# Three of four chunks of the experts' second layer by parts, one high part cast on GpSimd, and a tail that runs one unit later

## What is computed

```python
x = x + attention(layernorm(x))          # 16 heads, weights (eps + |q - k|)^-2, gated
x = x + experts(layernorm(x))            # 8 experts, top 2, 128 -> 512 -> 128, relu
x = x + linear_attention(layernorm(x))   # 16 heads of 8, relu(q), relu(k) with decay
x = x + f(layernorm(x))                  # 384 of 512 tokens: gelu(x @ w_block); the others: x itself
```

## Time and profile before

| | |
|---|---|
| median of 3 runs | 1418.41 us (1417.85 to 1419.69) |
| profiled execution | 1417.84 us, its span 1416.1 us |
| mean TensorE clock granted | 0.997 of full |
| busy: TensorE, VectorE, ScalarE, GpSimd | 1385.1, 1091.4, 1099.4, 840.5 us |

### The profile page before, as it was taken

How to read it: one execution, slowest core, us unless ns; L and a number is a source line. 1 busy time by engine, 2 the same in 40 slices (tenths; PEclk the granted TensorE clock), 3 DMA queues, 4 the chain that set the end, 5 groups by cost and what they waited for, 6 DMA issues and landing times.

```text
span 1416.1 us, 18228 instructions
## 1 busy us (share of the span) xinstructions
PE 1385.1 (98%) x6488; PEld 742.1 (52%) x6488; DVE 1091.4 (77%) x2045; ACT 1099.4 (78%) x947; POOL 840.5 (59%) x657
## 2 busy tenths in 40 slices
PE   8999999999999999999999999899999999999996
PEld 4444444444444444444444444445777777777775
DVE  7887897788888887887888778635687686776857
ACT  2799789979978979979979979944676676766761
POOL 4568777777778778868877877411333333434330
PEclk9999999999999999999999999999999999999999
DMA  3000110111101101101101012443011010110100
GB/s 114 1 17 16 31 39 17 23 31 32 25 16 46 24 17 36 34 17 31 39 16 32 16 25 58 124 143 107 1 68 56 12 68 1 68 61 8 68 1 16
DMA packets 45705, 54.99 MB, mean 39 GB/s; under 512 B 13808, under 2 KB 32368, under 8 KB 44464
## 3 DMA queue, kind: packets, MB, share of 16 engines
q1 hardware_dynamic: 45616, 53.84, 13.0%
HBM read 48.97 MB, written 4.85 MB: 38 GB/s over the span
## 4 chain that ended last, share of the span: by engine, by line
PE 86%; DVE 8%; ACT 5%; issue 1%; DMA 0%; POOL 0%; SPq 0%; DVEq 0%; POOLq 0%
PE sc L406 14%; PE av L419 13%; PE z L74 12%; PE pj L74 12%; PE y L1214 8%; PE sc L401 6%; PE y L74 5%; PE pj L383 4%; PE pj L451 4%; DVE w L597 3%; PE pj L429 2%; ACT w L684 1%; ACT w L688 1%; ACT w L680 1%; DVE high L565 1%
## 5 line engine op out<-in xcount | busy, mean ns | idle before, releaser
L597 DVE TENSOR_SCALAR w<-sc 128x1024 f32<-128x1024 f32 x256 | 301.3, 1218 | 67.7 <-PE sc L406 66.4
L680 ACT ACTIVATE w<-w 128x2048 f32<-128x2048 f32 x128 | 237.6, 1904 | 121.5 <-DVE w L597 121.2
L320 POOL TENSOR_TENSOR wsum<-wsum,w 128x512 f32<-128x512 f32 x248 | 318.0, 1282 | 19.4
L969 POOL TENSOR_TENSOR hr_l<-hr,hr_h 128x512 fp32r<-128x512 f32 x112 | 151.9, 1357 | 261.6 <-ACT hr L1025 261.6
L406 PE MATMUL sc<-query,key 64*128 64x512 f32 x1024 | 241.7, 591 | 0.0
L684 ACT ACTIVATE w<-w 128x2048 f32<-128x2048 f32 x128 | 240.1, 1899 | 0.4
L688 ACT ACTIVATE w<-w 128x2048 f32<-128x2048 f32 x128 | 239.8, 1897 | 0.0
L419 PE MATMUL av<-w,vt 128*64 128x512 f32 x1024 | 233.8, 598 | 2.5 <-ACT w L688 2.4
L1025 ACT ACTIVATE hr<-z,b 128x512 f32<-128x512 f32 x256 | 173.4, 684 | 67.7 <-PE z L74 67.7
L306 POOL TENSOR_TENSOR sqq<-query 128x512 f32<-128x512 f32 x63 | 65.6, 1042 | 182.8 <-DVE query L537 137.1
L317 POOL TENSOR_TENSOR wsum<-w 128x512 f32<-128x512 f32 x124 | 159.3, 1285 | 5.2 <-ACT w L688 5.2
(11 more groups left out here) (214 smaller groups left out, 2360.7 us busy)
## 6 DMA issues: line engine op xcount, KB each, us to landing
hT<-head_recips SPq DMA_DIRECT2D x64, 256.0 KB, 4.0
rb<-routing SPq DMA_DIRECT2D x8, 2048.0 KB, 7.1
w<-in_W SPq DMA_DIRECT2D x16, 256.0 KB, 5.4
xa<-in_X SPq DMA_DIRECT2D x8, 256.0 KB, 4.4
xc<-in_X SPq DMA_DIRECT2D x8, 256.0 KB, 2.8
x<-xc SPq DMA_DIRECT2D x8, 256.0 KB, 4.1
x<-x SPq DMA_DIRECT2D x1, 1792.0 KB, 7.9
out<-prod SPq DMA_DIRECT2D x7, 256.0 KB, 2.3
```

The source lines that it names most:

```text
L320: nc.gpsimd.tensor_tensor(wsum[:, u, :], wsum[:, u, :], w[:, j % 2, u, c, :], ALU.add).then_inc(s_added, 1)
L597: nc.vector.tensor_scalar(w[:, s, 2 * r:2 * r + 2, c, :], sc[:, i, :, :], 0.0, None, ALU.max).then_inc(s_d2, 1)
L680: nc.scalar.activation(w[:, j % 2, u, :, :], w[:, j % 2, u, :, :], ACT.Sqrt).then_inc(s_sqrt, 1)
```

## The change

The condition for a product by parts goes from "odd units" to all units but the first of each expert: three chunks of four. Of the middle one (k % 4 == 2, `by_pool`) ScalarE writes only `hr`, and GpSimd casts it to `hr_h` before it subtracts. The weights of three chunks per expert are split instead of two, and the splitting moves one unit later. The turn of the tail moves from unit 10 to 12 (of LATE from 8 to 10), qkv from 13 to 14, keys from 16 to 17, numerators from 18 to 19, the turn of o1 from 20 to 21, the second turn from 29 to 30, the scores from 29 to 31, and the turn of the routing from 24 to 26. On VectorE the ranks and the results go two units later, and `add_experts` with its statistics one unit earlier. The ranks share one scratch row, so each waits for the one before.

```diff
         def in_parts(n):
-            return n >= NU and n % 2 == 1
+            return n >= NU and n % NF > 0
+
+        def by_pool(n):
+
+            return in_parts(n) and n % NF == 2
...
-            for n in range(NU + 1, B * NU, 2):
-                m = n // 2
-                pool.wait_ge(S["hr"], n + 1)
-                nc.gpsimd.tensor_tensor(hrs[1][:, m % (HR // 2), :], hr[:, n % HR, :],
-                                        hrs[0][:, m % (HR // 2), :].bitcast(F32), ALU.subtract).then_inc(S["lo"], 1)
+            n_hi = 0
+            for n in range(NU, B * NU):
+                if in_parts(n):
+                    high, low = hrs[0][:, part(n) % HP, :], hrs[1][:, part(n) % HP, :]
+                    pool.wait_ge(S["hr"], n + 1)
+                    if by_pool(n):
+                        n_hi += 1
+                        nc.gpsimd.tensor_copy(high, hr[:, n % HR, :]).then_inc(S["hi"], 1)
+                        pool.wait_ge(S["hi"], n_hi)
+                    nc.gpsimd.tensor_tensor(low, hr[:, n % HR, :], high.bitcast(F32), ALU.subtract).then_inc(S["lo"], 1)
...
-                if in_parts(n):
+                if in_parts(n) and not by_pool(n):
                     if n == NU + 1:
                         act.wait_ge(att["x1_out"], 16 * B)
...
-                    if k == at(t, 10):
+                    if k == at(t, 12):
...
-                    if k == at(t, 13):
+                    if k == at(t, 14):
                         qkv(t)
...
-                    if k == at(t, 18):
+                    if k == at(t, 19):
                         numerators(t)
...
-                    if k == 24:
+                    if k == 26:
                         turn_routing(f)
...
                 if 0 <= u < B and u != LATE:
-                    if 2 <= k < 2 + NC:
-                        token_ranks(u, k - 2)
-                    if k == 7:
+                    if 4 <= k < 4 + NC:
+                        token_ranks(u, k - 4)
+                    if k == 9:
                         kept(u)
...
                 if 0 <= t < B:
-                    if k == 9:
+                    if k == 8:
...
-                    if k == (10 if t == LATE else 11):
+                    if k == (11 if t == LATE else 12):
                         tail_norm(t, 0)
...
-                if b == 0 and k >= 24:
-                    if k == 24:
+                if 25 <= n < 25 + NE:
+                    if n == 25:
```

More of the change, by code:

```diff
@@ L772, in psum @@
             return own.enter_context(nc.psum_tensor(name, shape, F32))
-        w1 = sb("w1", [P, NE, FF])
+        with ExitStack() as until_split:
+            w1 = until_split.enter_context(nc.sbuf_tensor("w1", [P, NE, FF], F32))
+        w2_l = sb("w2_l", [P, NE * (NF - 1), D], F32R)
+        scr = sb("scr", [P, 2, T])
         w2 = sb("w2", [P, NE * NF, D])
@@ L859, in build_rest @@
         N_F = 13
-        N_T, N_R = 11, 4
+        N_T, N_R = 14, 7
         LATE = B - 2
@@ L882, in res_of, with ranks_of @@
             return spare(1) if t == LATE else prod[:, :, :]
+        def ranks_of(t, c):
+            if t < LATE:
+                return scr[:, 0, :], scr[:, 1, 0:P]
+            return (scr[:, 0, :], scr[:, 1, :], rb0[:, 6, :], rb0[:, 7, :])[c], xn_f[:, c, :]
         def at(t, k):
@@ L1029, in step @@
                 if 0 <= u < B:
-                    if k == (0 if u == LATE else 3):
+                    if k == (0 if u == LATE else 4):
                         turned_t(u, 1)
@@ L1205, in expert @@
                     pe.wait_ge(S["rwT"], 1)
-                if n == NU + 1:
-                    pe.wait_ge(S["w2s"], NE * NF)
                 pe.wait_ge(S["hr"], n + 1)
                 if in_parts(n):
-                    pe.wait_ge(S["lo"], (n - NU) // 2 + 1)
-                    m = product(nc, y[:, g % 2, :], [w[:, k // 2, :] for w in w2s],
-                                [v[:, n // 2 % (HR // 2), :] for v in hrs], start=False, stop=(i == NF - 1))
+                    if b == 1 and i == 1:
+                        pe.wait_ge(S["w2s"], 2 * (NF - 1) * (k // NF + 1))
+                    pe.wait_ge(S["lo"], part(n) - part(NU + 1) + 1)
+                    m = product(nc, y[:, g % 2, :], [w[:, part(k), :] for w in w2s],
+                                [v[:, part(n) % HP, :] for v in hrs], start=False, stop=(i == NF - 1))
                 else:
@@ L1255, in step @@
                         idle(t, 12)
-                    if k == (26 if t == LATE else 29):
+                    if k == (26 if t == LATE else 30):
                         turn_t(t, 1)
@@ L1260, in step @@
                             processed(t)
+                    if k == (26 if t == LATE else 31):
                         scores(t)
@@ L1478, in split_w2 @@
             def split_w2(e):
[L1479 to L1484, removed]
+                parts = slice((NF - 1) * e, (NF - 1) * (e + 1))
+                source = w2[:, NF * e + 1:NF * (e + 1), :]
+                V.tensor_copy(w2s[0][:, parts, :], source).then_inc(S["w2s"], NF - 1)
+                dve.wait_ge(S["w2s"], (NF - 1) * (2 * e + 1))
+                V.tensor_tensor(w2s[1][:, parts, :], source, w2s[0][:, parts, :].bitcast(F32),
+                                ALU.subtract).then_inc(S["w2s"], NF - 1)
             def weigh(g):
```

55 lines of the change are left out of this document (28 added, 27 removed).

## The result

| | before | after |
|---|---|---|
| median | 1418.41 us (1417.37 to 1419.69, 5 runs) | 1431.28 us (1430.15 to 1432.82, 5 runs) |
| profiled span | 1416.1 us | 1430.9 us |
| ratio | | 1.0088, 95% interval 1.0076 to 1.0099 |

The account below looks back on a forecast made before the run. TensorE alone was taken to set the time. Terms -9.3 + 10.5 + 1.9 + 9.0 = +12.1 us on the profiled 1417.84 gave 1429.9, forecast as 1430; range 1409 to 1441 for 8 in 10, likeliest case 1420 to 1441.

Parts of the forecast that it names:

- TensorE, -9.3: Saving on TensorE: 56 chunks in blocks 1 to 7, each 0.17 us cheaper by parts, taken as -9.3 us.
- rival 1: VectorE's waits stay hidden and the kernel gets faster, 1408.5 us; chance 0.23, half-gains down to 1415.6 included.
- The cast, 1.0 us: GpSimd's new cast per expert, taken as 1.0 us between bounds of 0.42 (VectorE's cast) and 1.04 (GpSimd's square).
- an estimated 1424: The forecast time if the cast takes the skill page's 769 ns, each place then waiting some 0.5 us less.
- Place A: VectorE's stretch from turn_sum to front_stats: late 0.8 to 2.9 us per block, taken 2.1; blocks 2 to 6, +10.5 us.
- air: Time left for VectorE's waits before TensorE or ScalarE is late: 4.7 us at turn_sum to front_stats.
- Block 7, +1.9: Loss from turn_sum on in block 7, waits of 4.5 to 6.5 against 3.6 us left: +1.9 us (0.9 to 2.9).
- Place B: VectorE's stretch from divide to the root at unit 31: late 1.5 us in blocks 1 to 6, +9.0 us.
- The turn of the routing: At unit 26, expected to wait within the same delay as the stretch from divide to the root at unit 31.
- GpSimd's load: GpSimd's busy time in the blocks, forecast to show in the profile as some 290 us.
- Rival 3: GpSimd itself late for TensorE, each 0.2 us over per expert costing 11 us: 1441 us; chance 0.05.

Follow-up runs that it names:

- e4: The changed kernel with GpSimd's casts and subtractions on 32 of 512 columns: 1407.35 us, ratio 0.9918 to the kernel before.
- e9: The changed kernel with later results, the cast on ScalarE, and the tail's first root at unit 11 instead of 12: 1417.13 us, ratio 0.9988 to before.
- e10: The changed kernel with later results, the cast on ScalarE, and the tail's first root at unit 10 instead of 12: 1415.81 us, ratio 0.9977 to before.
- e8: The kernel before with each of GpSimd's 112 subtractions done twice, nothing of the change in it: 1444.9 us, ratio 1.0176 to before.

## Why the prediction was right

1430 was forecast and 1431.28 measured, and mostly by the steps that it gave.

- **TensorE, -9.3.** Right in its sum: from block 1 on, e4 is 9.3 us shorter than before. With GpSimd made nearly free the kernel gains 0.8%, which is rival 1's time (1408.5; measured 1407.35). In its parts it is somewhat off: the cheaper chunks give 1.3 us in a block, 8.3 in all, and the new places give 1.4 us that I had not counted.
- **The cast, 1.0 us.** Too high. It takes 0.61 us (602/612/1123 ns min/median/max), nearer to the lower bound. The Trainium skill, "GPSIMD Engine Reference", section 3.1, gives 769 ns for 512 elements; the trace shows less. By that page the sum was an estimated 1424, and still the higher sum came out: with the short cast the waits lay in the ranges that I had given for the long one. That the forecast lies within 2 us of the result is in part luck, a cast taken too long against losses taken too short.
- **Place A, late 2.1.** Measured 2.24, in blocks 2 to 6. The waits under it: keep 1.06, the results 3.52 - 1.14 = 2.4, tail_norm 4.48 - 4 x 0.34 = 3.1, together 6.5, where I had 5.5 to 7.6 against an air of 4.7. The difference, 1.8, leaves out what TensorE loses behind each of its waits.
- **Block 7, +1.9.** Too low: three late turns of 0.44 + 1.24 + 1.11 and 0.07 behind them, 2.9, at the upper end of its 0.9 to 2.9.
- **Place B, late 1.5.** Measured 1.54, six times. I had put it in blocks 1 to 6; in the trace it comes at the end of each and is counted in blocks 2 to 7. The waits: 0.54 + 0.34 + 1.08 + 1.08 + 0.87 = 3.9, where I had 3.5 to 4.7. The turn of the routing didn't wait.
- **Not foreseen:** ScalarE's first root of the tail, one unit later with its table load, makes a first layer start 0.37 us late. It costs 0.08 us six times, 0.5 in all. I had costed ScalarE at nothing because the number of relus is the same, and not looked at which unit the load stands in; here that was harmless, in e9 and e10 it was not.
- **GpSimd's load** was forecast at some 290 us in the blocks and is 241 in the 390 us shown, which hold 53 of the 56 casts; the short cast is most of the difference.
- **Rival 3**, GpSimd late for TensorE: didn't happen; no row of TensorE waits for `lo`.

The sum with the measured terms is -9.3 + 5 x 2.24 + 2.9 + 6 x 1.54 = +14.0; the -9.3 is e4's and holds the places and the 0.5 of the root. From block 1 on the spans differ by 14.3.

That VectorE waits for GpSimd's time is shown: e4 takes away, and e8 adds, hardly more than GpSimd's time, and VectorE's rows move with it. The Trainium skill, "SBUF — State Buffer", section Who interferes with whom, states that one of the two engines fully blocks the other. The rows agree with it (four operations in 4.48 us instead of 1.38); that the ports are the reason, no run here tests. What I had from the rows beyond the rule, that GpSimd gets in between back-to-back instructions, decided between 1408 and 1430.

Open: what the kernel would gain with B's last 0.40 us gone, which was not tried, and why TensorE loses another 0.1 us behind a wait.

## What to carry to other kernels

Moving work to an idle GpSimd isn't free for VectorE when both work in SBUF. Take GpSimd's whole work in the critical stretch as the most that VectorE can wait there, and compare it with the air of that stretch, not with the idle share of the engine: at place A VectorE waited 6.5 us in a stretch in which GpSimd had 8.9 us of work, and the air was 4.7. A short operation counts too: the eight casts of a block, 0.61 us each, made it 1.6 us longer. Before such a change, first take what isn't urgent out of the stretch: with the results moved, and the cast on ScalarE, the same saving of TensorE made the kernel 0.5% faster instead of 0.9% slower. And a row that starts late is not yet a loss: look at whether the row behind it is late too.

## What was not expected of the hardware

**The two engines don't share evenly.** GpSimd's pairs of subtractions took 2.59 and 2.53 us at place A, 1.3 us each, as when alone, while VectorE's eight operations of 0.3 us took 8.0 us in all; VectorE's came in between GpSimd's at the seams and hardly delayed it. Here the engine with few long operations keeps its pace, and the one with many short ones pays.

**The granted clock after a wait.** In e8 the turn of the routing waits six times for the ranks, each time 2.75 us or 0.01 less. Four of these rows of TensorE:

```profile
1036.29 1.02 PE L1112 MATMUL fa<-ident,rw 128*8 128x128 f32 x4 [2.75 <-DVE rw L1367]
1098.69 0.60 PE L1112 MATMUL fa<-ident,rw 128*8 128x128 f32 x4 [2.75 <-DVE rw L1367]
...
1220.63 1.02 PE L1112 MATMUL fa<-ident,rw 128*8 128x128 f32 x4 [2.75 <-DVE rw L1367]
1283.04 0.60 PE L1112 MATMUL fa<-ident,rw 128*8 128x128 f32 x4 [2.74 <-DVE rw L1367]
```

Twice the four small matmuls behind the wait took 1.02 us instead of 0.60, and there the granted clock is at its half level, 1.2 GHz. Windows of 3 us (busy us of PE, PEld, DVE, ACT, POOL; then the clock):

```profile
1217.00:1220.00 3.00, 0.89 (x4) 0.38 (x2) 2.83 (x7) 1.26 (x2) 1.89 (x2) 1.00 0.00 0
1220.00:1223.00 3.00, 2.37 (x7) 1.23 (x7) 2.92 (x12) 0.57 (x1) 1.79 (x2) 0.52 0.00 0
1223.00:1226.00 3.00, 3.00 (x13) 2.17 (x11) 0.73 (x4) 1.75 (x2) 0.00 (x0) 0.91 0.53 180
```

The clock fell some 0.5 us before the wait ended. It stayed down for 3.4 us each time, and block 4, which holds the second one, took 62.39 us instead of 61.0. The other four equal waits left the clock at 2.4 GHz. Why two and not the rest, the runs don't show; in before and after every 3 us of blocks 1 to 7 were at 1.00. So here a wait cost more than its length, twice in six.
